# Linear-attention layer with gated output on 8 Trainium2 cores: the final gate product is issued one step later on VectorE

## What is computed

```python
xn = layernorm(x)                       # x: (8, 2048, 1024), one (2048, 1024) per core
q, k, v = silu(xn @ Wq), silu(xn @ Wk), silu(xn @ Wv)
o = lightning_attn(q, k, v)             # chunks of 128, 16 heads of 64, decayed state kv
o = (o - mean(o)) * rsqrt(var(o) + 1e-5) * gamma + beta      # over the 1024 features
gate = sigmoid(xn @ Wg1 @ Wg2)
s = (o * gate) @ Wo
g = silu(xn @ (W + up_aux @ (lora_up @ (lora_down @ down_aux))).T + b)
y = x + s * g
```

## Time and profile before

| what | us |
|---|---|
| median of 2 runs (734.64 to 735.22) | 734.93 |
| the profiled execution | 735.51 |
| its span, on the slowest core (core 2) | 733.8 |
| spans of the other cores | 726.4 to 733.3 |
| VectorE busy in it | 300.1 (41%) |
| TensorE matmul busy in it | 510.7 (70%) |

### The profile page before, as it was taken

The page is one execution under the profiler, slowest core; times in us unless marked ns, Lnnn a source line. Parts: engine busy times, 40 slices in busy tenths (PEclk is TensorE's granted clock), DMA queues, the critical chain, the costliest instruction groups (busy, mean ns, idle before and its releaser), DMA issues.

```text
span 733.8 us, 8358 instructions; the slowest of 8 cores (726.4 to 733.8 us)
## 1 busy us (share of the span) xinstructions
PE 510.7 (70%) x2644; PEld 246.4 (34%) x2678; DVE 300.1 (41%) x611; ACT 209.1 (28%) x393; POOL 89.4 (12%) x76
## 2 busy tenths in 40 slices
PE   0118467999999961676666666999966767667663
PEld 0013233444444430444444451244432323232321
DVE  1360633110212004555555566100027778777773
ACT  0024333563333320333333322933321111111110
POOL 0000000000001001544445420000000000000000
PEclk9999687999999995656656575599988686877786
DMA  8780411000469973000000001410001322323313
GB/s 245 250 261 36 143 31 56 1 0 1 132 183 176 165 177 108 1 1 1 1 1 1 2 11 58 148 53 1 0 1 29 58 44 43 58 33 54 55 32 58
DMA packets 14048, 49.72 MB, mean 68 GB/s; under 512 B 3728, under 2 KB 3729, under 8 KB 13878
## 3 DMA queue, kind: packets, MB, share of 16 engines
q0 software_dynamic: 2448, 16.78, 13.6%
q1 hardware_dynamic: 9254, 24.02, 10.3%
q10 hardware_dynamic: 2304, 8.39, 3.8%
HBM read 40.79 MB, written 16.78 MB: 78 GB/s over the span
## 4 chain that ended last, share of the span: by engine, by line
PE 41%; DVE 22%; issue 9%; DMA 9%; ACT 8%; another core or an unknown queue 7%; DVEq 1%; SPq 1%; POOL 0%; ACTq 0%; POOLq 0%
PE pb L437 15%; PE pb L822 8%; DMA LANDB<-wq 4%; PE pb L938 3%; PE pb L654 2%; DVE CC L924 2%; DVE SAB L605 2%; DVE CC L918 2%; PE pb L641 2%; PE pb L809 2%; DVE RBI L913 2%; PE pb L661 2%; DVE CCo L924 2%; DMA LUPF<-lup 2%
## 5 line engine op out<-in xcount | busy, mean ns | idle before, releaser
L437 PE MATMUL pb<-XNT,WS 128*128 128x512 bf16 x500 | 116.8, 393 | 15.0 <-ACT XNT L487 14.2
L437 PEld LDWEIGHTS pb<-XNT,WS 128*128 128x128 bf16 x512 | 51.1, 101 | 78.4 <-issue 23.3
L641 PE MATMUL pb<-SAB,VO 128*128 128x256 bf16 x128 | 30.4, 355 | 58.2 <-DVE SAB L611 34.0
L403 DVE CAST WS<-LAND 128x1024 bf16<-128x1024 f32 x20 | 16.4, 821 | 122.1 <-DMA LAND<-w 52.8
L822 PE MATMUL pb<-WS,XNT 128*128 128x512 bf16 x251 | 59.4, 388 | 0.5 <-issue 0.3
L530 PE MATMUL pb<-WS,XNT 128*128 128x512 bf16 x251 | 55.3, 379 | 1.6 <-DVE WS L403 1.4
L481 PE MATMUL pb<-IDB,XNTM 128*128 128x128 bf16 x128 | 13.0, 262 | 60.8 <-DVE XNTM L470 36.4
L677 ACT ACTIVATE VO<-pb 64x256 bf16<-64x256 f32 x64 | 24.1, 377 | 109.3 <-PE pb L661 106.4
L667 POOL TENSOR_TENSOR KVBD<-KVBD,LAMCB 128x512 bf16<-128x512 bf16 x32 | 36.8, 1150 | 138.3 <-DVE KVBD L693 66.7
L938 PE MATMUL pb<-WS,CCo 128*128 128x512 bf16 x122 | 45.4, 540 | 7.1 <-DVE CCo L924 5.3
L938 PE MATMUL pb<-WS,CC 128*128 128x512 bf16 x123 | 44.8, 534 | 5.2 <-DVE CC L924 2.9
(11 more groups left out here) (93 smaller groups left out, 745.1 us busy)
## 6 DMA issues: line engine op xcount, KB each, us to landing
y<-SGT POOLq DMA_DIRECT2D x16, 512.0 KB, 5.3
XV<-x ACTq DMA_DIRECT2D x12, 512.0 KB, 13.0
XTS<-x ACTq DMA_DIRECT2D x4, 512.0 KB, 7.8
LAND<-wq SPq DMA_DIRECT2D x4, 512.0 KB, 5.7
LANDB<-wq SPq DMA_DIRECT2D x4, 512.0 KB, 5.7
LAND<-wk SPq DMA_DIRECT2D x4, 512.0 KB, 3.6
LANDB<-wk SPq DMA_DIRECT2D x4, 512.0 KB, 4.1
LAND<-wv SPq DMA_DIRECT2D x4, 512.0 KB, 3.5
```

What stands on the lines that cost most here:

```text
L437: p.pe(lambda e, k=k, oc=oc, t4=t4, bank=bank, wten=wten: e.matmul(PB[bank][:], wten[:, k * 1024 + oc * 128:k * 1024 + (oc + 1) * 128], XN ...
L641: p.pe(lambda e, pp=pp, c=c, ob=ob, ocol=ocol, w=w, i=i: e.matmul(PB[ob][:, ocol:ocol + 256], VO[:, c * 1024 + pp * 128:c * 1024 + (pp + 1 ...
```

## The change

The two L945 instructions and the L950 DMA of `p4c_S` move into a helper of their own, `p4c_G`. In the loop it is called for tile tc-1 after `p4c_B(tc)`; before, its instructions stood between `p4c_A(tc)` and `p4c_B(tc)`. TensorE's instructions keep their order. On VectorE the pair of tile tc-1 goes from ahead of L913 of tc to behind the 16 products of tc. On GpSimd's queue the DMAs keep their order among themselves.

```diff
@@ -940,6 +940,10 @@
                     WS1[:, ec * 1024 + h * 512:ec * 1024 + (h + 1) * 512],
                     start=(ec == 0), stop=(ec == 7)),
                     reads=[bCCP[par][ec], bWS1[ec]], writes=[bPB[sb0 + h]])
+
+    def p4c_G(tc):
+        par = tc % 2
+        sb0 = 4 + par * 2
         sgt, sgb = (SGT, bSG) if tc % 2 == 0 else (SGT2, bSG2)
         for h in range(2):
             p.dve(lambda e, tc=tc, h=h, sb0=sb0, sgt=sgt: e.tensor_tensor(
@@ -958,7 +962,9 @@
         p4c_A(tc)
         p4c_S(tc - 1)
         p4c_B(tc)
+        p4c_G(tc - 1)
     p4c_S(NTILE - 1)
+    p4c_G(NTILE - 1)
 
     p.final_wait(out_toks)
     p.replay()
```

## The result

| | before | changed |
|---|---|---|
| median of the runs, us | 735.0 | 762.9 |
| ratio, with its 95% interval | | 1.0374 (1.0356 to 1.0392) |
| profiled execution, its time and span, us | 735.51, 733.8 | 763.56, 761.7 |

The kernel is slower by 27.9 us by the medians, 3.7%. The forecast was 755.7 with a range of 752.5 to 762.0, so the direction came true and the size lies just above the range. Here is the page of the changed kernel: its first line, the granted clock in 40 slices, and two groups by line (count, then busy us and mean ns, then idle time before it and its releaser). The moved lines have new numbers: the pair is L949 and the DMA L954.

A forecast was written before the change was run, and what follows sets the result against it. The last stage was taken as bound by a chain of waits, mostly on VectorE, 11.21 us a tile, with the pair in a hole. 19.6 + 0 + 1.2 = 20.8 us on the median 734.93 gave 755.7, range 752.5 to 762.0.

The forecast's parts named there:

- the empty hole before L913: VectorE idles 1.73 us before L913, 1.13 at the smallest; taking the pair out of there gains nothing.
- Step 2: Between the last L924 and the next L884, each moved pair costs 1.40 us; 14 insertions make 19.6 us.
- Step 5: No wait is added; TensorE's output product gets 1.4 us more before L901 needs the engine and stays covered.
- the sum: Whole kernel: 19.6 for the insertions, 0 for the end, 1.2 for the last DMA, 20.8 us in all.
- a rival beside the forecast: TensorE's clock drops at L901 and L910 after longer idling: at most 7.4 us more, 763.1; chance 0.13.
- Step 4: The last two output DMAs meet; the last is pushed back 0 to 1.9 us, taken as 1.2.
- Step 3: At the end, tile 14's pair fits ahead of the last pair, which waits for TensorE: 0 to 0.1 us.
- L884 and GpSimd's issue: Rival: L884 and the DMA's issue hold each other, 12.0 us more, 767.7; chance 0.03.
- The other side: Rival: the pair, waiting for a late output product, was holding the reciprocal; moving it gives 736.1 or faster; chance 0.06.

The follow-up runs named there:

- Experiment 1: The kernel before, with the L945 pair written twice in a row at its old place ahead of L913: 737.8 us, ratio 1.0038.
- experiment 4: The changed kernel, with 6 unused matmuls a tile put on TensorE between each output product and L901: 758.0 us, ratio 1.0305.
- Experiment 6: The changed kernel, with tile 14's pair and DMA put back ahead of L913 of tile 15: 759.8 us, ratio 1.0344.
- experiment 7: The kernel before, with each feature block's first product (L918) issued ahead of the second (L924) of the block before: 712.9 us, ratio 0.9702.
- experiment 8: The kernel before with its 16 products interleaved, and in it the pair and DMA moved behind the products: 731.9 us, ratio 0.9950 to the kernel before.
- experiment 3: The kernel before, with only the pair's second half and the DMA moved behind the products: 746.9 us, ratio 1.0160.

## Why the prediction was wrong

**Where the pair stood, and where it went: right.** The chain, the empty hole before L913 and its 1.73 us were read rightly. Experiment 1 filled the hole a second time, for about 0.1 us a tile.

**Step 2, the price of an insertion and its count: right.** 1.40 us each and 14 of them were forecast. The timeline shows 1.39, and experiment 4, with the clock repaired, 12.68 - 11.29 = 1.39 over 14 tiles: 19.5 us.

**Step 5 and the sum: here it failed.** The sum carried TensorE's statistics at their old length. The step said only that TensorE's product stays covered, and that the clock would stay was the assumption behind it. The longer idle time of TensorE was seen, and made a rival beside the forecast with a chance of 0.13, when it should have been a term in the sum with both its ends. Against it the prediction held that the clock was back at its full level before L901; but that was read in a tile where TensorE idled 1.69 us there, and the change makes it up to 3.08. What the runs showed in place of nothing: 5 to 6 us, 6.2 on the profiled core by experiment 4. The measured 762.9 lies next to this rival's 763.1, but that nearness is luck. The clock took less than the rival's 7.4, and the last DMA more than the sum's 1.2.

**The size of that rival: too small.** The price of a slow tile, 0.53 us, was taken from the first tile, where L901 took 0.86 us because a piece of it ran at full clock. A whole L901 at half clock takes 1.01, and the waits beside it grow too: the slow tile above is 5.10 - 4.34 = 0.76 us longer. The upper end would have been 14 x 0.76 = 10.6 us and not 7.4. The range ended at 762.0, inside this rival's case, and so missed the result by 0.9 us.

**Step 4, the last DMA: right in kind, low in size.** It was given 1.2 us of a possible 1.9; from issue to the end it grew by 9.1 - 7.0 = 2.1. With the 1.4 us that lay between the two issues, the step's own upper end comes to 3.5 - 1.4 = 2.1, so the two did not overlap at all by that estimate. Experiment 6 shows that it was the meeting of the two.

**Step 3, the end of the compute: right.** The last two pairs ran in one piece of 2.87 us. From the start of the last L924 to the end of the last pair it is 752.04 - 748.90 = 3.14 us, and was 726.24 - 722.94 = 3.30, so nothing was lost there.

The sum as measured, set against the two profiled spans: 19.5 for the place, 6.2 for the clock, 2.1 for the last DMA make 27.8 of 761.7 - 733.8 = 27.9 us. That they agree so closely is luck. From the last L884 to the last issue it is 0.5 us more than before (15.3 against 14.8), and up to the second L884 it is 0.4 less (553.6 against 554.0), and the two nearly cancel.

**The other rivals.** L884 and GpSimd's issue don't hold each other: L884 lasts 1210 to 1220 ns with the issue beside it. The other side had its mechanism wrong: a late product holds L901 first, and a single pair is done before L910, as experiments 7 and 8 show. A look at TensorE's queue would have given that beforehand.

**The two rules.** With the Trainium skill's SBUF — State Buffer the trace agrees: the GpSimd issues, which now start beside L884, take 867 ns on average against 865, and L884 isn't longer. The section "HAM oscillation — how this bites in real kernels" of TensorE: Matmul & The Clock Gate, in the Trainium skill, was nearer to the truth than the weight I gave it. It says that bursts parted by waits meet the low clock. The trace agrees in many tiles of the changed kernel, such as the one at 591.85, and not in all, and the fillers of experiment 4 show that TensorE's idle time is the cause, as it says.

## What to carry to other kernels

Before moving an instruction, find the idle time that it now stands in and ask what the engine does at the new place: the same two products cost 0.1 us in one place and 1.4 in the other, and 1.8 with what they did to TensorE's clock. When a tile gets longer, every engine that isn't the bound idles longer. For TensorE that is a term of its own if short matmuls stand in the chain. Its lower end is nothing, as in experiment 8, and its upper end is to be taken from a row that runs at the low clock from start to end. Before calling a wait the bound, look at what else stands behind the same event. Here both the pair and the chain's matmuls waited for the output product, and the chain's way to the reciprocal, 1.8 us, was longer than the pair's 1.5.

## What the runs showed that I had not expected

The clock at L901 does not follow from the idle time just before it alone. In the changed kernel a tile with 3.08 us of TensorE idle time before L901 (at 581.7) had it at 0.61 us, and the one shown above, with 2.72, at 1.01. An idle time longer by 0.6 us (experiment 3) did almost no harm and one longer by 1.4 did, but in the interleaved kernel even that did none (experiment 8). What decides in the single tile was not tried.

Adding matmuls made a kernel faster: 90 whose result nobody reads saved 5 us in the changed kernel (ratio 1.0374 to 1.0305), and 45 in the kernel before did nothing (0.9997).

The interleaving of dependent VectorE pairs was worth more than the change cost: an instruction that reads the result of the one right before it started 0.45 us after it in place of 0.27, and 22 us hung on the order of the 16 products.
